# Transformer block with windowed attention and a top-2 mixture of experts: a reordered seam between attention and expert 0, and a last group finished tile by tile

## What is computed

```python
h = _layernorm(x) * (1 + ca) + sa
x = x + ga * attention(h, Wqkv, Wout)      # 16 heads of 64, causal window of 128, softmax
h = _layernorm(x) * (1 + cb) + sb
# mixture of experts: E = 8, FF = 1024, K = 2 choices, CAP = 640 slots per expert and choice
probs = softmax(h @ gate_w.T + gate_b); topk_prob, topk_idx = top_k(probs, K)
for c in range(K):
    pos = cumsum(one_hot(topk_idx[:, c]))[...] - 1; keep = pos < CAP
    xbuf[idx * CAP + pos] = h                       # scatter into the expert's slots
    hid = relu(xb @ W1[e] + b1[e]); yb = hid @ W2[e] + b2[e]
    y += yb[slot] * prob * keep                     # gather back
x = x + gb * y
```

## Time and profile before

| | us |
|---|---|
| median of 3 runs | 1110.84 |
| lowest and highest | 1109.87, 1111.73 |
| the profiled execution's own time | 1115.25 |
| its span, first to last instruction | 1113.5 |
| TensorE busy | 1052.4 (95%) |
| VectorE busy | 782.7 (70%) |
| ScalarE busy | 662.8 (60%) |
| GpSimd busy | 499.0 (45%) |

### The profile page before, as it was taken

The page is one execution under the profiler, slowest core; times in us unless marked ns, Lnnn a source line. Parts: engine busy times, 40 slices in busy tenths (PEclk is TensorE's granted clock), DMA queues, the critical chain, the costliest instruction groups (busy, mean ns, idle before and its releaser), DMA issues.

```text
span 1113.5 us, 28021 instructions
## 1 busy us (share of the span) xinstructions
PE 1052.4 (95%) x10746; PEld 726.7 (65%) x10746; DVE 782.7 (70%) x1746; ACT 662.8 (60%) x1930; POOL 499.0 (45%) x546
## 2 busy tenths in 40 slices
PE   6989999999999999999979878899999999999995
PEld 3456766766666766667656555568585858586765
DVE  5677767778788787786777975557665757576653
ACT  4677667567567666666664846445646472837460
POOL 2244445456366364464463574432525252435342
PEclk9999999999999999999999998999999999999998
DMA  9544101221132031032022034553535253536000
GB/s 321 114 161 155 45 21 35 44 62 40 38 72 42 7 85 28 18 75 62 29 58 69 23 117 109 96 135 88 114 111 102 95 106 115 105 116 87 15 21 10
DMA packets 140173, 87.59 MB, mean 79 GB/s; under 512 B 96756, under 2 KB 130698, under 8 KB 139916
## 3 DMA queue, kind: packets, MB, share of 16 engines
q1 hardware_dynamic: 129292, 64.29, 23.0%
q0 software_dynamic: 10752, 21.54, 7.1%
HBM read 40.02 MB, written 33.79 MB: 66 GB/s over the span
## 4 chain that ended last, share of the span: by engine, by line
PE 83%; DVE 6%; ACT 4%; issue 4%; POOL 1%; DMA 0%; SPq 0%; another core or an unknown queue 0%; ACTq 0%; DVEq 0%; POOLq 0%
PE down L1846 18%; PE up L1832 18%; PE gen L667 14%; PE gen L787 7%; PE score L704 7%; PE gen L681 6%; PE gen L714 5%; PE pv L746 4%; PE pv L736 2%; ACT prob L1034 2%; DVE prob L1257 1%; DVE negmax L1249 1%; ACT norm_space L1058 1%; DVE score L1245 1%; ACT packed L1064 0%
## 5 line engine op out<-in xcount | busy, mean ns | idle before, releaser
L1874 ACT ACTIVATE hid<-up,b1T 128x512 f16<-128x512 f32 (+2 forms) x192 | 122.8, 640 | 181.8 <-PE up L1832 166.0
L1832 PE MATMUL up<-xT,w 128*128 128x512 f16 (+2 forms) x1152 | 212.8, 346 | 8.3 <-issue 8.3
L1846 PE MATMUL down<-w,hid 128*128 128x256 f16 x1920 | 214.6, 274 | 4.7 <-DVE hid L1890 4.7
L1647 POOL TENSOR_SCALAR_AFFINE_SELECT probT_split<-probT_split 128x512 f32<-128x512 f32 x128 | 112.5, 879 | 234.0 <-ACT probT_split L1043 233.3
L1846 PEld LDWEIGHTS down<-w,hid 128*128 128x128 f16 x1920 | 189.1, 99 | 29.7 <-DVE hid L1890 5.2
L667 PE MATMUL gen<-hT,big 128*128 128x512 f16 x768 | 187.3, 383 | 3.2 <-ACT probT_split L1043 2.6
L1034 ACT ACTIVATE prob<-score,negmax 128x128 f32<-128x128 f32 x512 | 181.1, 376 | 7.2 <-DVE negmax L1249 7.1
L1832 PEld LDWEIGHTS up<-xT,w 128*128 128x128 f16 x1152 | 112.8, 98 | 102.7 <-issue 10.8
L1890 DVE TENSOR_TENSOR hid<-hid 128x512 f16<-128x512 f32 (+2 forms) x192 | 115.2, 606 | 89.3 <-ACT hid L1875 63.7
L1933 POOL DMA_INDIRECT out<-y,tail x80 | 81.9, 1024 | 210.4 <-DVE y L1918 197.5
L667 PEld LDWEIGHTS gen<-hT,big 128*128 128x128 f16 x768 | 74.7, 99 | 85.2 <-ACT probT_split L1043 6.8
(11 more groups left out here) (168 smaller groups left out, 1651.6 us busy)
## 6 DMA issues: line engine op xcount, KB each, us to landing
big<-in_L_ffn_W SPq DMA_DIRECT2D x14, 1024.0 KB
slot_inputs<-empty_row SPq DMA_DIRECT2D x80, 129.5 KB, 2.4
out<-x SPq DMA_DIRECT2D x7, 512.0 KB
k<-k SPq DMA_DIRECT2D x48, 64.0 KB, 1.8
x<-in_L_attn_x SPq DMA_DIRECT2D x4, 512.0 KB, 4.2
x<-in_L_attn_x SPq DMA_DIRECT2D x2, 1024.0 KB, 14.4
kept<-out,tail POOLq DMA_INDIRECT x80
out<-y,tail POOLq DMA_INDIRECT x80
```

The source lines that it names most:

```text
L1647: pool.affine_select(out=own, in_=whole, pattern=[[0, TILES], [-1, P]], compare_op=ALU.is_gt, fill=zero, base=0, channel_multiplier=1).the ...
L1832: mm = pe.matmul(bank, w1[:, par, kd, a, ft * P:(ft + 1) * P], part_rows(e, n, xT[:, par, b * KD + kd, :]), start=(i == 0), stop=(i == 5))
L1846: mm = pe.matmul(down[n][:, s, :], hid[:, ft, a, t * P:(t + 1) * P], w2[:, par, ft, b, :], start=(i == 0), stop=(i == 3 * FT - 1))
L1874: act.activation(part_rows(e, n, hid[:, ft, 0, :]), bank, ACT.Relu, scale=1 / W_SCALE, bias=bias).then_inc(hid_hi, 1)
```

## The change

Four edits. Line numbers in the diff are those of the code, and functions and tables keep their names.

1. **The early half's chain.** VectorE's modulate goes ahead of the normalise of the same step, its low part ahead of the next step's softmax work; ScalarE's pack goes directly behind the exponentials. TensorE's transposes move from step 17 to 16, logits from 18 to 17, and counts get a step of their own, 18. The eighth own send moves from step 19 to step 16.
2. **The late output pair.** It sums in `late_pair`, two 256-column halves of different banks of `score[0]`, whose last user is unit 14, and its products are spread: head pairs 0 to 2 in step 16, 3 and 4 in step 18, 5 and 6 and then 7 at the end. VectorE reads it from there, and TensorE's first up product waits for that (`late_taken`), since the up banks lie in the same place. In the first up parts of expert 0 the late half's logits come behind product 3 (before, 5) and its counts behind product 6 (before, 9).
3. **Expert 0's third up part** goes behind two down groups instead of three; VectorE's finishes follow, and its later weight splits go behind the hid blocks on both ScalarE and VectorE.
4. **The last group** of the last expert is summed in two banks (its second tile in `up[0]`), finished and sent tile by tile.

```diff
-            EARLY_AT = {"add": 14, "stats": 14, "rstd": 15, "modulate": 15, "pack": 16, "low": 16, "turn": 17, "logits": 18}
-            LAST_OWN_SENDS = {13: (0, 1), 14: (1, 3), 15: (3, 5), 16: (5, 7), 19: (7, 8)}
+            LATE_AT = (16, 18)
+            EARLY_AT = {"add": 14, "stats": 14, "rstd": 15, "modulate": 15, "pack": 16, "low": 16, "turn": 16, "logits": 17, "counts": 18}
+            LAST_OWN_SENDS = {13: (0, 1), 14: (1, 3), 15: (3, 5), 16: (5, 8)}
-            NEXT_SPLIT = [13, 15, 22, 23]
+            NEXT_SPLIT = [13, 15]
...
+            late_pair = score[0][:].rearrange("p t q -> p (t q)").rearrange("p (s n) -> p s n", s=2)[:, :, 0:D]
...
+                    def late_products(c, units, pairs):
+                        pe.wait_ge(attn_lo, H * c + units)
+                        for t in (2, 3):
+                            mm = project_out_tile(c, late_pair[:, t - 2, :], t, pairs)
+                        return mm
...
-                            if i == STEPS[-1]:
-                                pe.wait_ge(attn_lo, H * c + H - 2)
-                                late, late_full = claim(c, ("out", 1))
-                                project_out_tile(c, half_bank(late, 2), 2, range(PAIRS - 2))
                             weighted_values(c, i - HI_AT)
+                            if i == LATE_AT[0]:
+                                pe.wait_ge(exp_done, H * c + H - 1)
+                                late_products(c, H - 5, range(3))
+                            if i == LATE_AT[1]:
+                                late_products(c, H - 3, range(3, 5))
...
-                        route_counts(NC)
-                        pe.wait_ge(attn_lo, H * c + H - 1)
-                        project_out_tile(c, half_bank(late, 2), 2, [PAIRS - 2])
-                        project_out_tile(c, half_bank(late, 3), 3, range(PAIRS - 1), opens=False)
-                        pe.wait_ge(attn_lo, H * c + H)
-                        for t in (2, 3):
-                            mm = project_out_tile(c, half_bank(late, t), t, [PAIRS - 1])
-                        mm.then_inc(late_full, 1)
+                            if i == EARLY_AT["counts"]:
+                                route_counts(NC)
+                        late_products(c, H - 1, range(5, PAIRS - 1))
+                        late_products(c, H, [PAIRS - 1]).then_inc(late_full, 1)
...
                         pe.wait_ge(w_lo, 4)
+                        pe.wait_ge(late_taken, 1)
                         pe.wait_ge(xT_first[0], 16)
...
-                        for g in range(3):
+                        for g in range(2):
                             down_product(pe, 0, 0, g)
                         pe.wait_ge(xT_first[2], 32)
                         for ft in range(FT):
                             up_product(pe, 0, 0, 2, ft)
-                        for g in range(3, DG):
+                        for g in range(2, DG):
                             down_product(pe, 0, 0, g)
...
-                            softmax_step(c, i, True)
+                            if i == EARLY_AT["low"]:
+                                route_low(dve, NC)
+                            if i == EARLY_AT["modulate"]:
+                                merge(c, i)
+                                row_max(c, i)
+                                part_modulate(NC)
+                                invert_sum(c, i - 1)
+                                normalise(c, i - 1)
+                            else:
+                                softmax_step(c, i, True)
...
+                        dve.wait_ge(late_full, 1)
+                        dve.scalar_tensor_tensor(gated[:], late_pair, 1 / W_SCALE, modrow[:, batch(c), 0:1, :].to_broadcast([P, 2, D]),
+                                                 ALU.mult, ALU.mult).then_inc(late_taken, 1)
...
+            def finish_end(dve, e, par, g):
+
+                n = (par * DG + g) % 2
+                at_least(dve, y_sent[n], 32 * ((DG * e + g) // 2))
+                for s, t in enumerate(pair_tiles(e, g)):
+                    dve.scalar_tensor_tensor(gate_row[:, n, s, :], gate_step[:, 0, :], second[:, par, t:t + 1],
+                                             modrow[:, 0, 3, :], ALU.mult, ALU.add).then_inc(end_gate, 1)
+                dve.wait_ge(kept_read[g], 32 * (e + 1))
+                dve.wait_ge(end_gate, 2)
+                for s, t in enumerate(pair_tiles(e, g)):
+                    m = t // (ST // K)
+                    dve.wait_ge(end_down, s + 1)
+                    dve.scalar_tensor_tensor(y32[:, n, s, :], end_bank(n, s), 1 / W_SCALE, b2B[:, e, :], ALU.mult, ALU.add).then_inc(end_made, 1)
+                    dve.wait_ge(end_made, s + 1)
+                    dve.scalar_tensor_tensor(y32[:, n, s, :], y32[:, n, s, :], tail[:, par, t, TAIL_GATES].bitcast(F32)[:, m:m + 1],
+                                             gate_row[:, n, s, :], ALU.mult, ALU.mult).then_inc(end_scaled, 1)
+                    dve.wait_ge(end_scaled, s + 1)
+                    dve.tensor_tensor(y32[:, n, s, :], y32[:, n, s, :], kept[:, g, s, :], ALU.add).then_inc(end_ready, 1)
...
+            def send_end(pool, e, g, par):
+
+                n = (par * DG + g) % 2
+                for s, t in enumerate(pair_tiles(e, g)):
+                    stand_ge(pool, (end_ready, s + 1))
+                    pool.indirect_dma_start(
```

More of the change, by code:

```diff
@@ L1849, in down_product, with end_bank, down_end @@
                 mm.then_inc(down_full, 1)
+            def end_bank(n, s):
+                return down[n][:, 0, :] if s == 0 else up[0][:, 0:D]
+            def down_end(pe, e, par, g):
+                n = (par * DG + g) % 2
+                pe.wait_ge(hid_ready, 4 + UG * e + (pair_part(e, g) + 1) * FT)
+                pe.wait_ge(y_ready, DG * e + g + 1)
+                for s, t in enumerate(pair_tiles(e, g)):
+                    i = 0
+                    for ft in range(FT):
+                        for a, b in SPLIT_PRODUCTS:
+                            mm = pe.matmul(end_bank(n, s), hid[:, ft, a, t * P:(t + 1) * P], w2[:, par, ft, b, :],
+                                           start=(i == 0), stop=(i == 3 * FT - 1))
+                            i += 1
+                    mm.then_inc(end_down, 1)
```

72 lines of the change are left out of this document (47 added, 25 removed).

## The result

| | before | changed |
|---|---|---|
| median of 6 runs each, us | 1111.28 | 1105.76 |
| lowest and highest | 1109.87, 1114.72 | 1103.88, 1107.30 |
| ratio, 95% interval | | 0.9939 [0.9923, 0.9955] |
| profiled execution: own time, span | 1115.25, 1113.5 | 1105.67, 1103.9 |

By the ratio, which is worked out from all runs and is not the quotient of the two medians (these lie 5.5 us apart), the change gives 0.61% (6.8 us; 5.0 to 8.6), not the 10.3 of the forecast; 1105.76 lies above the range of 1098.2 to 1103.8. Two more comparisons gave 0.9934 [0.9914, 0.9954] and 0.9942 [0.9916, 0.9967].

What follows compares the result with a forecast made beforehand. The bound was taken to be TensorE, full in experts 1 on, with the seam from last attention chunk to expert 0 (649 to 736 us) bad. Parts 1 to 4 gave 8.1, part 5 2.2: 1110.84 - 10.3 = 1100.5; range 1098.2 to 1103.8.

Steps and rivals of the forecast that it cites:

- Part 4: Expert 0's third up part behind two down groups: removes the 4.75 us hole and saves 2.5 on the 13.07 behind it.
- the holes are waits and full-speed products, so I carry the 10.3 over whole: Whole kernel: gain worked out on the profiled execution applied unchanged to the median, 1110.84 to 1100.5 us.
- Part 1: Early half's chain in the last attention chunk: its first send leaves earlier, gain 1.4 to 1.5 us, bounds 0 and 3.
- I expect the 2.4 GHz level to hold there: TensorE's new hole at about 655.4 to 658.05, ahead of unit 14's values: no clock fall.
- some 5 us of nearly full work: TensorE's work ahead of the new hole before unit 14's values, given as reason for the clock to hold.
- rival B: Seam: clock falls in the new hole, among other losses; price 1 to 2.5 us, 1101.5 to 1103; 0.24 with another rival.
- the trace shows no hole like the new one: Clock argument for unit 14's hole: trace agrees with the skill's rule for the 4.75 us hole, but has none similar.
- 2 us to spare: Early half's one-hot, said to have this slack, as an argument against the seam giving only part.
- Part 2: Output pair in the score bank: late products end at 663.7, not 665.02; no product added, added waits cost nothing.
- Part 3: Late logits and counts inside expert 0's first up part: loss 0.5 us, late rows land at about 699.4.
- Part 5: Last expert's last group by tiles: end comes 0.95 + 1.29 = 2.2 us nearer to TensorE's end.

Runs made afterwards that it cites:

- x2: Kernel before with only the third up part behind two down groups and the last group by tiles: 1107.82 us, ratio 0.9944.
- x9: Kernel before with only the third up part behind two down groups, on another chip: 1101.93 us (before 1107.00 there), ratio 0.9949.
- x10: Changed kernel with the third up part back behind three down groups, on another chip: 1104.42 us, ratio 0.9970 to the kernel before.
- y4: Changed kernel without the last group by tiles, on the first group's chip: 1108.63 us, ratio 0.9960 to the kernel before.
- x4: Changed kernel with late head pairs 3 and 4 moved to step 17, behind the early half's logits: 1105.89 us, ratio 0.9925.
- x11: Changed kernel with the eighth own send behind the last split, late logits behind up product 5, counts behind 9; another chip: 1098.73 us, ratio 0.9921.
- x8: Kernel before with the last group by tiles and nothing else: ratio 0.999 [0.9972, 1.0009].
- the second group: Four follow-up runs: kernel before unchanged, two own sends behind the last split, late counts behind product 8, last group by tiles alone; ratios 1.000, 0.9922, 0.9932, 0.999.
- x3: Changed kernel with the eighth own send back behind the last split (step 19): 1104.00 us, ratio 0.9914.
- x5: Kernel before, unchanged, for a second trace: ratio 1.000 [0.9985, 1.0015].
- y2: Kernel before, unchanged, its fourth trace, on the first group's chip: 42.60 us from first down group to expert 1; no ratio given.
- the third group: Four follow-up runs on another chip, of kernels with single parts added or undone or the eighth own send put back: ratios 0.9949, 0.9970, 0.9921, 0.9922.

## Why the prediction was wrong

**Part 4, the term that was mis-sized.** The mechanism was right: no idle ahead of the third up part or the fourth down group, 36.56 from the first down group to expert 1 in eleven traces of kernels with part 4 (37.95 in the twelfth, x2). The price was 7.15, and the profiled pair shows 7.33. But I took it from one execution. Six traces with the old order gave 43.89, 39.69, 45.00, 39.70, 43.81 and 42.60: mean 42.4, so part 4 is worth 3.1 to 8.4 and 5.9 on average. By times it is 5.6 where it stands alone (x9) and about 3.5 where it is the last to come (x10 against the changed kernel, across chips). The step that failed is "the holes are waits and full-speed products, so I carry the 10.3 over whole". The profiled execution was 4.4 us above the median, and its excess sat partly in the very hole that I priced: ScalarE's idle of 1.57 at 716.33, and the low clock behind the hole. A hole of 2.96 at full speed would have been the other end of the range (3.1), and the forecast 10.3 - 4.2 = 6.1 us of gain, 1104.7.

**Part 1.** The moved send did what the forecast said on GpSimd: the split of unit 14 ended 1.2 later, counted from v, and TensorE's hole was 2.20. The step that failed is "I expect the 2.4 GHz level to hold there". Its premise, "some 5 us of nearly full work" ahead of the hole, did not come either: 2.5 us of work stood there, behind an idle of 1.27 (650.18 to 652.69 in the changed kernel). The clock fell in four of five traces with three own sends in step 16 and this order (2.50 to 2.74 for the 12 products, against 1.49 in y4). That was rival B, with a price of 1.7 and too small a chance. The forecast also said that the trace shows no hole like the new one. It does, four us ahead of the place, unit 13's values in the kernel before:

```profile
652.91 1.03 PE L773 MATMUL pv<-probT_split,v 128*64 128x256 f32 x4 [1.98 <-POOL probT_split L1647]
```

They took 1.03 for the 0.65 of full speed: this hole stands just ahead of the 0.51 of the earlier trace rows, with the clock at 1.00 up to it. The fall came there in five of seven traces with the old early chain. The forecast had set a rule against it, the Trainium skill's "TensorE: Matmul & The Clock Gate", "HAM oscillation — how this bites in real kernels". What that section describes are waits of 3 to 5 us between bursts, longer than this hole, so the forecast stretched it: it does not cover a hole of 2.20, and yet the clock fell behind one in four traces of five.

In the traces with the fall A is 19.39 to 20.20, about the same as before the change. Where the clock held (y4) A was 18.65: 1.2 of the forecast's 1.4 to 1.5 were there, with the send in step 16. So the fall took nearly all of part 1's gain. VectorE came out otherwise too, without cost here. The one-hot was forecast 13.5 us behind v (658.1) and was ready at 15.9 (657.44), by 1.4 of idle ahead of the logits and the longer operations shown above. The "2 us to spare" of rival B were gone, but in the changed kernel the counts could come no earlier anyway, because 12 products stand ahead of them (657.90 against 657.96 in y4). Where the hole is filled or shorter, VectorE is the gate: the counts waited 1.53 in x4 and 0.69 with the send put back, where A is 17.92, 18.05, 18.26 and 18.27, a gain of 1.6 to 1.9.

**Part 2.** Its products cost nothing; expert 0 never waited for VectorE's reading of the bank.

**Part 3.** The one-hot wait was to rise from 0.78 to 1.3. It is 1.25, 1.51 and 1.59 in three traces of the changed kernel and 0.78, 0.88, 0.54 and 0.55 in four of before: a rise of 0.8, not 0.5. The stretch rose by 0.9 on average (19.66 to 20.57), with the clock's recovery behind the first up products scattering it by 1.2. What part 3 may buy is safety: with the old places the rows were 1.22 late in x2, but in time in x9 and x11; why they were late only once was not looked into.

**Part 5.** 2.2 forecast, 2.26 by the means of four and three traces (11.34, 9.08).

**The parts together.** By the traces they give 0 - 0.9 + 5.9 + 2.3 = 7.3 us where the forecast had 10.3: 1.5 less by the clock in part 1, 1.2 less by the hole in part 4, 0.4 less by part 3.

**Not in the sum.** Two stretches that no part touches moved. First, the start: v is 644.2 to 645.4 in four traces of before and 641.5 to 642.2 in three of the changed kernel. Of that, 1.6 us is a fall of the clock behind a wait of 2.13 or 2.14 at 65 us, which both have. Windows of before, then of x2:

```profile
66.00:68.00 2.00, 2.00 (x27) 1.87 (x27) 1.83 (x6) 0.72 (x3) 0.00 (x0) 0.50 0.42 144
```

```profile
66.00:68.00 2.00, 2.00 (x18) 1.08 (x20) 2.00 (x5) 1.14 (x3) 0.86 (x2) 1.00 0.43 146
```

It fell in the four traces of before and in x8, x9 and x10, and in none of the eleven others, with the same instructions ahead of it. It repeats with the program and with none of the parts; the cause is open. Second, the seven experts took 366.8 before and 367.8 changed (means), by ScalarE gaps of mostly 1.6 to 3 us that leave TensorE without its bank; with none of them it is 365.3. Whether the change adds to these is open too.

The means of the traces come to 9.2 in all, but for rounding (2.9 start, 0 part 1, -0.9 part 3, 5.9 part 4, -0.9 experts, 2.3 end). The three comparisons give 6.8, 7.4 and 6.5 us by their ratios, 6.9 on average, each with an interval of 1.8 to 2.8 to either side. Single executions of before in the second group run from 1110.6 to 1120.2, and the four profiled ones of before lie 1.6 us above the medians of their comparisons on average (the first 4.0), the three of the changed kernel 0.6 below. These 2.2 are the difference; whether it is chance isn't shown. So it is in part luck that the parts' 7.3 lies so near to the measured 6.8: what stands outside them (+2.9, -0.9, -2.2) happens to cancel. Likewise x9's 5.6 is 2.5 more than its trace explains; its profiled execution took 1104.98, 3 us more than its median.

## What to carry to other kernels

Where the profiled execution is slower than the median, look for the excess before pricing anything: an idle whose releaser was long done may sit inside the very hole that the change removes, and then the hole has a range and not a value. An edit that moves one DMA to the front of a full queue can cost more through TensorE's clock than through the queue (in A, 0.7 to 1.6 us against 0.4 to 0.7, the latter by y4 against the four traces with the send put back): compare the hole that it opens with holes of the same length elsewhere in the trace (here 1.98 us, four us ahead, with the low clock behind it). And when a gate is moved, ask for the third one: the own send cost in step 16, cost behind the split as a pair, and cost nothing that was seen there alone.

## What the runs showed of the hardware

- **VectorE beside GpSimd.** The subtraction of two small SBUF operands (128x16) took 0.18 us with GpSimd idle and 1.49 in x3, from 652.93 to 654.42; GpSimd's run of four splits ended at 654.38. Rows of x3, VectorE and GpSimd:

```profile
652.93 1.49 DVE L1340 TENSOR_TENSOR logit<-logit,lmax 128x16 f32<-128x16 f32 x1
```

```profile
653.73 0.65 POOL L1672 TENSOR_SCALAR_AFFINE_SELECT probT_split<-probT_split 128x512 f32<-128x512 f32 x1
```

  The Trainium skill ("GPSIMD Engine Reference", "Specifications") says that GpSimd's SBUF interfaces are shared with VectorE, with contention for instructions of two SBUF inputs; the trace agrees. In x3 it ended only with the run of splits. In the changed kernel it took 0.84 (654.57 to 655.41) and ended inside the run, which lasted until 655.95, so how long it waits varies.
- **The take of the logits.** With three own sends in step 16 VectorE idled 1.37 to 1.41 us ahead of them, past the end of the products, in five of the six such traces (not in x10), and never with a send put back. The cause was not found.
- **The clock behind short holes.** Behind 2.20 or 2.21 us ahead of unit 14's values it fell to 0.50 four times of five; behind 0.92 it held in four of four; behind 1.97 to 1.99 it fell five times of seven; behind 2.96 it held in x5 and x10 and fell in y2.
- **ScalarE gaps.** Idles of mostly 1.6 to 3 us (one of 3.76 in y4) with the input ready came in the experts in every trace but the four of the third group, on whose chip the kernel before took 1107.0 instead of 1111.3 to 1114.7. Their cause was not tried.
